# A fused GNN, Mamba and expert kernel: decays moved to PSUM, B and C copies in one bank, one bank of row sums

## The reference

```
# edges: attention sums over the edges of each target node
e = leaky_relu(s_src[src] + s_tgt[tgt]);  exp_e = exp(e - max)
denom = segment_sum(exp_e, tgt)
agg = segment_sum(proj[src] * attn, tgt)
# Mamba over the nodes in order of degree: 256 channels x 16 states
dt = softplus(...);  A = -exp(A_log)
dA = exp(dt[:, :, None] * A)                 # decay
dBx = (dt * xc)[:, :, None] * Bm[:, None, :] # inflow
h = dA_t * h + dBx_t ;  y_t = h @ C_t        # scan over nodes, read out
# then gates, feed-forward, layer norms, and an expert layer
```

## Time and profile before

| | |
|---|---|
| median of 3 runs | 3835.91 us (3835.72 to 3837.45) |
| the profiled execution | 3837.54 us, its span 3835.8 us |
| busy share of the span | PE 75%, DVE 70%, POOL 69%, ACT 56% |
| mean granted clock of PE | 0.896 of full speed |
| the loop of the scan, 940 to 2880 us: busy of 1940 us | DVE 1733, PE 1595, POOL 1538, ACT 1378 |
| gathers in the loop (L565) | 1344, mean 1151 ns |

### The profile page before, as it was taken

One profiled execution on the slowest core, in us unless ns is written; L12 is line 12 of the kernel. 1 busy time (PEld: TensorE's weight loads), 2 busy tenths in 40 slices (PEclk: granted clock), 3 DMA queues, 4 the chain that ended last, 5 costly groups with the idle time before them and its releaser, 6 DMA issues. The chain is left out here.

```text
span 3835.8 us, 60997 instructions
## 1 busy us (share of the span) xinstructions
PE 2892.4 (75%) x16306; PEld 2167.6 (57%) x16307; DVE 2685.3 (70%) x4282; ACT 2147.8 (56%) x4790; POOL 2659.7 (69%) x2148
## 2 busy tenths in 40 slices
PE   6465576527788788887887888888883888659998
PEld 5455455415565565565665655655652454448887
DVE  7577566625998888889988888899883788511111
ACT  2322377716777677677676676776772666412222
POOL 2688788877777777777777777777774477424443
PEclk8788767767999999999999999999996999879999
DMA  6433434454444444444444444444456233157665
GB/s 210 114 84 83 134 105 107 116 169 133 122 123 117 125 118 117 126 119 120 122 118 120 123 117 122 119 116 127 119 116 140 51 108 102 68 133 143 143 143 105
DMA packets 291620, 460.16 MB, mean 120 GB/s; under 512 B 55256, under 2 KB 213705, under 8 KB 291113
## 3 DMA queue, kind: packets, MB, share of 16 engines
q0 software_dynamic: 116320, 279.61, 30.7%
q1 hardware_dynamic: 175048, 178.02, 16.0%
HBM read 394.01 MB, written 63.43 MB: 119 GB/s over the span
## 5 line engine op out<-in xcount | busy, mean ns | idle before, releaser
L565 POOL DMA_INDIRECT el_g<-table,el_ix x1344 | 1547.4, 1151 | 407.3 <-issue 394.2
L681 PE MATMUL fl_ps<-el_g,el_oh 128*128 128x260 f32 x3520 | 986.7, 429 | 251.9 <-DVE el_g L608 203.4
L681 PEld LDWEIGHTS fl_ps<-el_g,el_oh 128*128 128x128 f32 x3520 | 715.0, 214 | 371.3 <-DVE el_g L608 210.9
L565 POOL DMA_INDIRECT el_g<-table,eg_src x436 | 590.4, 1354 | 155.9 <-issue 126.7
L608 DVE TENSOR_TENSOR el_g<-el_g,fl_pw 128x1024 f32<-128x1024 f32 x440 | 533.6, 1213 | 17.4 <-ACT fl_pw L652 17.4
L1110 DVE TENSOR_TENSOR_SCAN mb_h<-mb_dA,mb_zero,mb_dB 128x900 f32<-128x900 f32 x224 | 468.1, 2090 | 45.4 <-issue 17.8
L1241 ACT ACTIVATE mb_dA<-mb_dt,mb_a 128x224 f32<-128x224 f32 x900 | 382.8, 475 | 60.3 <-DVE mb_dt L1155 35.4
L1364 PE MATMUL fl_py<-mb_hc,ident 128*128 128x448 f32 x896 | 394.3, 563 | 0.5 <-DVE mb_hc L1120 0.5
L626 ACT ACTIVATE el_away<-el_dst,el_less 128x512 bf16<-128x512 bf16 x445 | 321.1, 722 | 107.5 <-DMA el_dst<-dst_rows 80.4
L641 ACT CAST el_oh<-fl_ptx 128x512 f32<-128x512 bf16 x444 | 253.2, 570 | 214.7 <-PE fl_ptx L668 210.7
L2247 POOL DMA_INDIRECT out<-ex_y,ex_to x112 | 174.1, 1554 | 278.2 <-DVE ex_y L2206 253.5
(11 more groups left out here) (307 smaller groups left out, 5504.0 us busy)
## 6 DMA issues: line engine op xcount, KB each, us to landing
el_dst<-dst_rows SPq DMA_DIRECT2D x446, 128.0 KB, 3.4
ex_w<-in_moe_W SPq DMA_DIRECT2D x56, 512.0 KB, 3.4
el_g<-table,el_ix POOLq DMA_INDIRECT x1344
ex_x<-routed_x SPq DMA_DIRECT2D x56, 257.0 KB, 2.7
el_g<-table,eg_src POOLq DMA_INDIRECT x436
mb_x<-sorted_x SPq DMA_DIRECT2D x30, 224.0 KB
table<-px_tr SPq DMA_DIRECT2D x7, 910.0 KB, 8.2
el_g<-in_x SPq DMA_DIRECT2D x7, 896.0 KB, 7.8
```

The source lines that it names most:

```text
L565: pool.indirect_dma_start(out=G[b // GU][:, b % GU * NJ + j, :], out_offset=None, in_=dram["table"], in_offset=bass.IndirectOffsetOnAxis(a ...
L681: mm = nc.tensor.matmul(pS[n % 2], OH[:, n % (2 * GU), j, :], G[n // GU % 2][:, n % GU * NJ + j, :], start=j == 0, stop=j == NJ - 1)
```

## The change

Three edits, which together leave the number of banks at eight.

1. The decays of a pair of states go to PSUM (`pA`, two banks) and no longer to SBUF. There is room for one pair of states only, where `dA` held two. So ACT makes all the decays of the next pair in the odd slot, behind the scan of the current pair, and in the even slot none. The taps of the convolution, which used to share `dA`, get a tile of their own.
2. The copies of B and C share one bank, `pBC`, in turn: copies_b waits until read_out has read the copies of C, copies_c until inflow has read those of B.
3. The row sums of the edges have one bank: gather_sums of a pair waits for the add of the pair before, where it waited for the one before that. PE does the edges of a slot first and the copies after them.

```
-        pS = [ps(f"fl_ps{b}", [P, 512])[:, 0:ROW] for b in range(2)]
+        pS = ps("fl_ps", [P, 512])[:, 0:ROW]
...
-            if not early(q, 2):
-
-                pe.wait_ge(s["added"], q - 1)
+            if not early(q, 1):
+
+                pe.wait_ge(s["added"], q)
...
-            dA = sb("mb_dA", [P, 4, KD, 1 + TC])
+            taps = sb("mb_taps", [P, CONV, D])[:]
-            pB, pC = ps("fl_pb", [P, 2, TC]), ps("fl_pc", [P, 2, TC])
+            pBC = ps("fl_pbc", [P, 2, TC])
+            pA = ps("fl_pa", [P, 1024])[:, 0:2 * KD * (1 + TC)].rearrange("p (s k t) -> p s k t", s=2, k=KD)
...
-                    nc.vector.tensor_tensor_scan(line(H[:]), line(dA[:, n % 2 * 2:n % 2 * 2 + 2]), line(dB[:]), ZERO[:, 0:1],
+                    nc.vector.tensor_tensor_scan(line(H[:]), line(pA), line(dB[:]), ZERO[:, 0:1],
...
-                    if not early(m, 4):
-
-                        act.wait_ge(s["h"], two_states(p).number - 1)
+                    if not early(m, 2):
+
+                        act.wait_ge(s["h"], two_states(p).number)
...
-                        ins = nc.scalar.activation(dA[:, n % 4, k, 1:], DT[:, n // NS % 2, k, :], ACT.Exp,
+                        ins = nc.scalar.activation(pA[:, n % 2, k, 1:], DT[:, n // NS % 2, k, :], ACT.Exp,
...
-                    decay(M + 2)
+                    if at % 2:
+                        decay(M + 1)
+                        decay(M + 2)
...
-                        pe.wait_ge(s["dB"], m)
+                        pe.wait_ge(s["hc"], m)
...
-                    if not early(m, 1):
-                        pe.wait_ge(s["hc"], m)
+                    pe.wait_ge(s["dB"], m + 1)
...
+                    if S:
+                        edges_tensor(pe, S)
                     if at % 2:
                         copies_b(two + 1)
                     else:
                         copies_c(two)
-                    if S:
-                        edges_tensor(pe, S)
```

More of the change, by code:

```diff
@@ L617, in add @@
             dve.wait_ge(s["summed"], q + 1)
-            nc.vector.tensor_tensor(at, at, pS[p.n % 2], ALU.add).then_inc(s["added"], 1)
+            nc.vector.tensor_tensor(at, at, pS, ALU.add).then_inc(s["added"], 1)
         def one_hot(act, p):
@@ L676, in gather_sums @@
             pe.wait_ge(s["turned_sb"], q + 1)
-            if not early(q, 2):
-                pe.wait_ge(s["added"], q - 1)
+            if not early(q, 1):
+                pe.wait_ge(s["added"], q)
             for j in range(NJ):
-                mm = nc.tensor.matmul(pS[n % 2], OH[:, n % (2 * GU), j, :], G[n // GU % 2][:, n % GU * NJ + j, :],
+                mm = nc.tensor.matmul(pS, OH[:, n % (2 * GU), j, :], G[n // GU % 2][:, n % GU * NJ + j, :],
                                       start=j == 0, stop=j == NJ - 1)
@@ L940, in streams @@
             DTR = sb("mb_dtr", [BX, TC])
-            dA = sb("mb_dA", [P, 4, KD, 1 + TC])
             dB, H = (sb(f"mb_{n}", [P, 2, KD, 1 + TC]) for n in ("dB", "h"))
             HC = sb("mb_hc", [P, 2, 2, KD, TC])
-            taps = dA[:].rearrange("p b k t -> p (b k t)")[:, 0:CONV * D].rearrange("p (j d) -> p j d", j=CONV)
+            taps = sb("mb_taps", [P, CONV, D])[:]
             XN = [t.rearrange("p b k t -> p (b k t)")[:, u * D:(u + 1) * D] for t in (dB[:], H[:], HC[:, 0]) for u in range(3)]
@@ L1085, in _ @@
                 dve.wait_ge(s["set"], 11)
-                nc.vector.memset(dA[:, :, :, 0:1], 0.0).then_inc(s["set"], 1)
+                nc.vector.memset(pA[:, :, :, 0:1], 0.0).then_inc(s["set"], 1)
                 def inflow(p):
@@ L1096, in inflow @@
                     wide_u = U[:, n // N2 % 2].unsqueeze(1).to_broadcast([P, 2, KD, TC])
-                    nc.vector.tensor_tensor(dB[:, :, :, 1:], wide_u, pB[:].unsqueeze(2).to_broadcast([P, 2, KD, TC]), ALU.mult
+                    nc.vector.tensor_tensor(dB[:, :, :, 1:], wide_u, pBC[:].unsqueeze(2).to_broadcast([P, 2, KD, TC]), ALU.mult
                                             ).then_inc(s["dB"], 1)
@@ L1119, in read_out @@
                         dve.wait_ge(s["y"], m - 1)
-                    nc.vector.tensor_tensor(HC[:, n % 2], H[:, :, :, 1:], pC[:].unsqueeze(2).to_broadcast([P, 2, KD, TC]), ALU.mult
+                    nc.vector.tensor_tensor(HC[:, n % 2], H[:, :, :, 1:], pBC[:].unsqueeze(2).to_broadcast([P, 2, KD, TC]), ALU.mult
                                             ).then_inc(s["hc"], 1)
@@ L1339, in copies_b @@
                     if not early(m, 1):
-                        pe.wait_ge(s["dB"], m)
+                        pe.wait_ge(s["hc"], m)
                     for r in range(2):
-                        mm = nc.tensor.matmul(pB[:, r, :], SEL[:, 2 * (n % N2) + r, :], PARTS[:, n // N2 % 2, :],
+                        mm = nc.tensor.matmul(pBC[:, r, :], SEL[:, 2 * (n % N2) + r, :], PARTS[:, n // N2 % 2, :],
                                               start=True, stop=True, skip_group_check=True)
@@ L1348, in copies_c @@
                     m, n = p.number, p.n
-                    if not early(m, 1):
-                        pe.wait_ge(s["hc"], m)
+                    pe.wait_ge(s["dB"], m + 1)
                     for r in range(2):
-                        mm = nc.tensor.matmul(pC[:, r, :], SEL[:, NS + 2 * (n % N2) + r, :], PARTS[:, n // N2 % 2, :],
+                        mm = nc.tensor.matmul(pBC[:, r, :], SEL[:, NS + 2 * (n % N2) + r, :], PARTS[:, n // N2 % 2, :],
                                               start=True, stop=True, skip_group_check=True)
```

## The result

The changed kernel takes 4121.1 us (median of 4 runs, 4118.1 to 4126.7) against 3836.7 for the kernel before, run beside it (3835.7 to 3840.5): ratio 1.0737, 95% interval 1.0723 to 1.0751. I forecast 4015, 3890 to 4110. So it is 284 us slower where I had 179: the direction was right, the size was not, and it fell just outside the range.

A forecast was written before the change was run, and what follows sets the result against it. DVE was taken as pacemaker (89% busy in the loop), with POOL close behind. Terms of 6.4 us per chunk, 28 times, made 179 us on 3837.5, less 1.6: 4015 us, range of 8 in 10 from 3890 to 4110.

The forecast's parts named there:

- at full clock it costs nothing more: Single bank of row sums, edges before copies: inflow 2.98 us from the add, against 3.01 by way of read_out.
- the second rival: PE idles before gather_sums and its clock falls; slots 3, 9, 15 go like slot 13: about 4145 us, chance 0.14.
- Slots 4 to 6: copies_c ahead of PE's convolution waits for slot 3's inflow, so the scan comes later: 1.7 us per chunk.
- Slot 15: Shared bank of B and C: inflow starts 0.46 after read_out instead of -0.08, 0.54 us lost.
- Slots 6 to 8: Scan of slot 8 waits longer for ACT, +0.75; scaling of slot 7 loses its wait, -0.6: 0.15 us per chunk.
- Slot 3: PE comes late, starting 1.06 instead of 0.48 behind the add; with the round trip's 0.54, 1.1 us.
- Slot 9: Only the copies' round trip between read_out and inflow counts, with nothing on DVE to hide it: 0.54 us.
- Slot 13: PE idles until the add, then does edges and copies at clock 0.58; 4.57 against 2.47: 2.1 us.
- the first rival: POOL was the bound: faster gathers win and round trips hide in DVE's idle time; about 3735 us, chance 0.09.
- Decays in PSUM: Scan reading an operand from PSUM and ACT writing there change nothing: 0, at most 7 us gained.
- Gathers: POOL's gathers may win up to 284 us when scans no longer hold them, costed at 0 since DVE paces.
- Decays single: Four decays in odd slots: +0.75 at slot 8's scan, -0.6 at slot 7's scaling, +0.3 in slots 1 and 11.

The follow-up runs named there:

- The long body alone: Changed kernel with a loop body of 64 slots and 48 edge pairs in place of 32 and 24 (6 turns, not 13): 4074.0 us, ratio 1.0624.
- the first experiment: Changed kernel with the single pair of decays back in SBUF, not PSUM, still written in odd slots: 4137.2 us, ratio 1.0787.

## Why the prediction was right in direction and short in size

Two steps failed. The first is "at full clock it costs nothing more", by which I priced slot 9 at 0.54 us and slot 7 at nothing: PE was not at full clock there. The second is a term that I put at nothing without a reason, the turn of the loop. In their place the runs show 1.12 us per chunk above my term in slot 9, 0.87 in slot 13 and 1.65 around the turn; PE kept at work takes 123 us off, and seven turns fewer 47. The 4121 lies nearer to the second rival's 4145 than to my forecast, but this is partly luck: that rival had slots 3, 9 and 15 at the lower clock, and of these only slot 9 was.

- *DVE paces and its path now holds round trips to PE*: right. Idle ahead of inflow stands at 321.5 us, DVE's share is 78%; I said about 82%.
- *Slots 4 to 6*, 1.7: measured 1.73. *Slot 15*: inflow 0.56 behind read_out where I had 0.46, and 0.65 of loss without a turn where I had 0.54. The rest of the excess in its interval is the turn.
- *Slots 6 to 8*, 0.15: 0.25, but by another way. The wait of the scaling went, as worked out (0.48 on average to 0). The scan of slot 8 was to wait about 1 us for ACT and waits 0.39 (0.32 before). Instead inflow of slot 7, which I had hidden behind the preparation, waits 0.80 for its copies, since gather_sums is slow there, and this covers most of ACT's lateness. With PE kept at work, and with the decays alone, the scan does wait 1.0 to 1.1 us: the term was right and the near agreement of the whole is luck.
- *Slot 3*, 1.1: 1.59 in the interval. Inflow is 0.92 behind read_out (median), 1.0 late, as worked out, and the rest is cold runs behind a turn.
- *Slot 9*, 0.54: 1.66. Here the forecast failed: I had put the clock into the second rival, as one case in seven. It came true in slots 7 and 9, and not in 3 and 15, where PE has worked until shortly before. With PE kept at work the interval is 8.13, 0.65 above the kernel before, so at full clock the step is right to 0.1.
- *Slot 13*, 2.1: 2.97. The mechanism was right and its size not: I took 3.14 us from a stretch with a mean clock of 0.58, which was not wholly at the lower level. After 5.3 us of idle in place of 4.12 the clock is 0.50 throughout, and gather_sums takes 3.80.
- *The turn of the loop*: no term at all. I had read DVE's slots in the middle of a body. Intervals 0 to 2 and 14 to 16 are 0.71 + 0.94 = 1.65 per chunk above my terms, 46 us in all. The long body alone won 47 with 7 of the 12 turns, so some of the turn's cost lies in other slots too.
- By the intervals: clock (8 to 10 and 12 to 14) 1.12 + 0.87, turn 1.65, slots 2 to 4 0.49, less 0.58 in 10 to 12 where I had a cost and there was a gain: 3.6 of the 3.7 us missed per chunk. The two of the clock make 56 us, less than the 123 that the added work wins, for that also takes back what I had priced as slow in slot 13 (about 1.6 us per chunk) and some of the cold runs behind a turn.
- The gain in slots 10 to 12: before, logits of slot 11 wait 0.31 us for gathers, on average, and now not at all. So DVE did wait for gathers, which my reading of the earlier trace rows against the first rival had denied; but only 8 times in the loop, 8.5 us in all. It goes with the longer chunk and not with the faster gathers, since the interval is 10.02 with the slow ones of the first experiment too.
- *Decays in PSUM*, 0: the scan takes 2087 ns against 2090, and the ACT instruction 436 ns on average against 471 in the same order into SBUF. Right, with the 16 us of the first experiment open.
- *Gathers*, 0: right. They went from 1151 to 960 ns and nobody gained. The first rival (POOL as the bound) is out. A scan with one operand in PSUM doesn't hold the gather beside it, and one with both in SBUF does; so the rule that I weighed (the Trainium skill, SBUF — State Buffer, § Who interferes with whom) is right about the scan's operands. Whether descriptor generation is left alone, as the page infers, isn't settled by it: these gathers also read their row numbers (`el_ix`) from SBUF, and no run takes the two apart.
- *Decays single*, +0.45 per chunk: alone they cost 1.6 (44 us). I priced ACT's queue at the scan and the scaling, not at keep_turned, on which PE's string of slots 1 to 5 hangs. In the whole change this error did not show, because that string is late anyway.

## What to carry to other kernels

A bank that is given up turns an engine that ran ahead into one that answers. Price that answer at the clock which the engine has after the new wait, and look at the turn of the loop, where queues lose their head start, as a slot of its own. Parts that delay the same string of work don't add: here 401 us of parts made 302. And where the engine that answers cools down while it waits, useless work in its idle time can win much (123 us here), but only if what follows is on the path (0 us in the kernel before).

## What I had not expected of the hardware

- The idle just before does not settle how slow gather_sums is. In the changed kernel 41 of them have 4.2 to 5.6 us of idle ahead, and took 3.4 to 3.8 us. Of 55 with 2.3 to 2.6 us ahead, 30 took 1.99 and the others up to 3.7 (the 3.09 above is one). With less than 1 us ahead they took at most 2.0, but for one case. At full clock it takes 1.92 to 1.99.
- The added matmuls (5.43 us for seven of 448 columns) cost DVE nothing: the next gather_sums started 0.57 us behind its add, as without them.
- The gathers' mean is 1130 to 1178 ns in all 15 kernels here whose decays lie in SBUF and 960 to 968 in the three others.
